# Second layer of a four-layer kernel: a quarter of the row maxima from half sums and half differences of the keys

## What is computed

```python
x_n = layernorm(x) * ln_gamma + ln_beta
q, k, v = split(x_n @ W_qkv + b_qkv)            # 16 heads of 8
scores = einsum('bhqd,bhkd->bhqk', q, k) * SCALE
scores = scores - max(scores, axis=-1)
attn = exp(scores)
attn = attn / maximum(sum(attn, axis=-1), 1e-12)
out = einsum('bhqk,bhkd->bhqd', attn, v) @ W_proj + b_proj
```

## Time and profile before

| | us |
|---|---|
| median of three runs | 3675.79 (3672.70 to 3679.34) |
| profiled execution, its own time | 3687.74 |
| its span in the profile | 3685.8 |
| `project` of the second layer, first load to barrier | 912.1 to 976.7 |
| slots ahead of the first step | 976.7 to 1028 |
| interleaved steps of the second layer | 1028 to 1686 |

### The profile page before, as it was taken

One profiled execution on the slowest core, in us unless ns is written; L12 is line 12 of the kernel. 1 busy time (PEld: TensorE's weight loads), 2 busy tenths in 40 slices (PEclk: granted clock), 3 DMA queues, 4 the chain that ended last, 5 costly groups with the idle time before them and its releaser, 6 DMA issues. The chain is left out here.

```text
span 3685.8 us, 51694 instructions
## 1 busy us (share of the span) xinstructions
PE 3002.9 (81%) x18320; PEld 1216.2 (33%) x18320; DVE 2627.6 (71%) x6022; ACT 2152.2 (58%) x2736; POOL 454.1 (12%) x601
## 2 busy tenths in 40 slices
PE   2699998787699999996599989986458988989836
PEld 1133333343212222223355555554332222222214
DVE  4688884456699999984566666641578888888831
ACT  2266665221267777785255545442259999989822
POOL 3000000323200000000000000002231010101023
PEclk9699998898689999998699999987779999999968
DMA  6422320422521121100000000011264222221102
GB/s 238 123 47 49 51 33 5 89 47 50 184 50 30 35 39 30 30 2 4 30 1 1 1 7 1 7 52 41 72 150 57 32 28 31 28 38 22 52 16 79
DMA packets 168110, 173.42 MB, mean 47 GB/s; under 512 B 46648, under 2 KB 126280, under 8 KB 165296
## 3 DMA queue, kind: packets, MB, share of 16 engines
q1 hardware_dynamic: 163760, 162.38, 20.2%
q0 software_dynamic: 4096, 7.78, 0.6%
HBM read 107.71 MB, written 62.26 MB: 46 GB/s over the span
## 5 line engine op out<-in xcount | busy, mean ns | idle before, releaser
L1205 ACT ACTIVATE a_probs<-a_scores 128x1024 f32<-128x1024 f32 (+3 forms) x896 | 793.1, 934 | 386.1 <-PE a_scores L1102 228.8
L1228 DVE TENSOR_REDUCE a_part_max<-a_slot_ps 128x1 f32<-128x512 f32 x1280 | 798.5, 683 | 44.9 <-PE a_slot_ps L1080 43.8
L1080 PE MATMUL a_slot_ps<-a_k_op,a_q_op 48*128 48x512 bf16 (+3 forms) x1792 | 585.4, 380 | 122.9 <-DMA a_mask_wide<-in_mask_wide 32.3
L2225 DVE TENSOR_TENSOR a_probs<-a_logit_ps,a_gate 128x1024 f32<-128x1024 f32 x512 | 602.4, 1219 | 102.6 <-ACT a_gate L2084 97.1
L2089 ACT ACTIVATE a_probs<-a_probs 128x2048 f32<-128x2048 f32 x256 | 488.0, 1906 | 9.4 <-DVE a_probs L2225 7.8
L1102 PE MATMUL a_scores<-a_q_op,a_k_op 51*128 51x512 bf16 (+3 forms) x1792 | 439.7, 362 | 18.5 <-ACT a_probs L1205 16.0
L1122 PE MATMUL a_o_ps<-a_probs,a_v_op 128*32 128x512 f32 (+3 forms) x3584 | 438.7, 561 | 1.2 <-ACT a_o_sb L1192 0.6
L1080 PEld LDWEIGHTS a_slot_ps<-a_k_op,a_q_op 48*128 48x128 bf16 x1792 | 149.7, 94 | 682.3 <-DVE a_part_max L1228 471.6
L1990 PE MATMUL a_logit_ps<-space 96*128 96x512 bf16 x1024 | 302.7, 386 | 75.3 <-DVE a_probs L2225 65.6
L2084 ACT ACTIVATE a_gate<-a_diff_ps 128x1024 f32<-128x1024 f32 x256 | 261.4, 1021 | 58.4 <-PE a_diff_ps L1990 49.9
L2003 PE MATMUL a_o_ps<-a_probs,a_v_op 128*32 128x512 f32 x2048 | 274.9, 608 | 7.0 <-DVE a_o_sb L2218 3.1
(11 more groups left out here) (389 smaller groups left out, 3791.1 us busy)
## 6 DMA issues: line engine op xcount, KB each, us to landing
scratch_v<-p_vpad SPq DMA_DIRECT2D x16, 1024.0 KB, 7.6
a_v_op<-scratch_v SPq DMA_DIRECT2D x32, 512.0 KB, 6.0
e_coef<-coef_dram SPq DMA_DIRECT2D x16, 1024.0 KB, 9.7
a_q_op<-scratch_q SPq DMA_DIRECT2D x384, 32.0 KB
a_k_op<-scratch_k SPq DMA_DIRECT2D x384, 32.0 KB
scratch_q<-p_parts SPq DMA_DIRECT2D x24, 384.0 KB, 4.5
scratch_k<-p_parts SPq DMA_DIRECT2D x24, 384.0 KB, 5.1
space<-scratch_k SPq DMA_DIRECT2D x192, 32.0 KB
```

What stands on the lines that cost most here:

```text
L1080: nc.tensor.matmul(out[:, 0:width], q_op[g][r0:r0 + MAX_ROW, e, qt * P:(qt + 1) * P], k_op[g][r0:r0 + MAX_ROW, e, kh * CH:kh * CH + width] ...
L1205: nc.scalar.activation(probs[gs % NB][:, 2 * e:2 * e + 2, off:CH], scores[e][:, :, off:CH], ACT.Exp, scale=scale).then_inc(probs_done, 1)
L1228: nc.vector.tensor_reduce(part_max[u % 2][:, kh, col:col + 1], slot[:, 0:w], axis=AX.X, op=ALU.max).then_inc(slot_done, 1)
L2225: nc.vector.tensor_tensor(probs[gs % 4][:, m, :, :], logit_ps[m][:], gate[gs % 2][:], op) \
```

## The change

In 8 of the 32 row tiles of a unit (odd head of the pair, odd `qt`; so slots B and D of every second group) the two slots are no longer the scores against the two halves of the keys. `project` computes two more operands for each batch element, (k of half 0 + k of half 1)/2 and their half difference, by two accumulating matmuls each with the k weights times 0.5 and -0.5, splits them into three parts like k and stores them in `scratch_halves`. `load_qk` loads them, 12 more DMAs for a unit. Slot B is now queries by half differences; ScalarE writes its absolute value to `sizes` in SBUF and frees the bank (`size_done`), VectorE passes over it. Slot D is queries by half sums; VectorE adds the sizes and takes the maximum in one `tensor_tensor_reduce`. The larger of two numbers is their half sum plus the size of their half difference, so the maximum over 1024 keys is the same. The first layer passes no `halves` and keeps its instructions, but for a wider preset of `part_max` and one wait in `project` that names a later chunk.

```diff
+    items = [(c, kind) for c in range(CHUNKS) for kind in ("qksd" if halves is not None and c % 2 else "qk")]
...
+                    else:
+                        te.wait_ge(halved, 2)
+                        nc.tensor.matmul(item_ps[n % NB][:], w_half[0][:], xnT[(c - 1) % 4][:], start=True, stop=False)
+                        nc.tensor.matmul(item_ps[n % NB][:], w_half["sd".index(kind)][:], xnT[c % 4][:], start=False, stop=True) \
+                            .then_inc(item_ready, 1)
...
+            if self.halves is not None:
+                for i in range(2):
+                    src = self.halves[b, i, kp, g * 32:(g + 1) * 32, :].rearrange("(e h r) t -> h r e t", e=2, h=2)
+                    r0 = HALF_ROWS + n * 8
+                    sp.dma_start(self.k_halves[g][r0:r0 + 8, i, :, :], src[1, :, :, :]).then_inc(self.qk_loaded[g], 16)
...
             def bank_for(n):
                 if n >= BANKS:
-                    te.wait_ge(slot_done, n - BANKS + 1)
+                    apart, count = shape.released[n - BANKS]
+                    te.wait_ge(size_done if apart else slot_done, count)
...
+            def slot_sizes(todo):
+
+                for u, s in todo:
+                    n = shape.place["slot", u, s]
+                    apart, count = shape.released[n]
+                    if apart:
+                        act.wait_ge(slot_ready, n + 1)
+                        if count > 2:
+                            act.wait_ge(slot_done, shape.released[shape.place["slot", *pairs[count - 3]]][1])
+                        nc.scalar.activation(sizes[(count - 1) % 2][:], slot_ps[n % BANKS][:], ACT.Abs).then_inc(size_done, 1)
...
                     for e in range(2):
+                        slot_sizes(todo[cut[2 * e]:cut[2 * e + 1]])
                         act.wait_ge(scores_ready, gs * 2 + e + 1)
...
+                        slot_sizes(todo[cut[2 * e + 1]:cut[2 * e + 2]])
...
+                if shape.in_pair(s):
+                    count = pairs.index((u, s)) + 1
+                    dve.wait_ge(size_done, count)
+                    nc.vector.tensor_tensor_reduce(out=slot[:], in0=slot[:], in1=sizes[(count - 1) % 2][:], scale=1.0,
+                                                   scalar=-3e38, op0=ALU.add, op1=ALU.max,
+                                                   accum_out=part_max[u % 2][:, kh, col:col + 1]).then_inc(slot_done, 1)
+                    return
```

More of the change, by code:

```diff
@@ L162, in _ @@
                 b, half = c // 2, c % 2
-                for i in range(ITEMS):
-                    n = c * ITEMS + i
+                for n in of_chunk[c]:
+                    kind = items[n][1]
+                    if kind in "qk":
+                        dram = (qs if kind == "q" else ks)[b, :, :, half * CH:(half + 1) * CH]
+                    else:
+                        dram = halves[b, "sd".index(kind)]
                     sp.wait_ge(lo_done, n + 1)
-                    sp.dma_start((qs, ks)[i][b, :, :, half * CH:(half + 1) * CH].rearrange("k f t -> f k t"),
-                                 parts[n % (2 * NB)][:]).then_inc(stored[n % (2 * NB)], 16)
+                    sp.dma_start(dram.rearrange("k f t -> f k t"), parts[n % (2 * NB)][:]).then_inc(stored[n % (2 * NB)], 16)
                 sp.wait_ge(v_done, c + 1)
@@ L171, in _ @@
                 if c == 3:
-                    for i in range(4):
-                        sp.wait_ge(stored[i], 16)
+                    for n in of_chunk[0] + of_chunk[1]:
+                        sp.wait_ge(stored[n], 16)
                 if c >= 3:
@@ L176, in _ @@
             for i in range(2 * NB):
-                sp.wait_ge(stored[i], 16 * (CHUNKS * ITEMS // (2 * NB)))
+                sp.wait_ge(stored[i], 16 * (len(items) // (2 * NB)))
             for i in range(4):
@@ L259, in _ @@
                 nc.gpsimd.memset(vp[:, :, :, hd:hd + 1], 1.0).then_inc(v_preset, 1)
-            for n in range(CHUNKS * ITEMS):
+            if halves is not None:
+                pool.wait_ge(loaded, 16 * n_loads)
+                for i, factor in enumerate((0.5, -0.5)):
+                    nc.gpsimd.tensor_scalar(w_half[i][:], w_qk[1][:], factor, None, ALU.mult).then_inc(halved, 1)
+            for n in range(len(items)):
                 pool.wait_ge(mid_done, n + 1)
@@ L899, in __init__, with in_pair, apart @@
         self.n = len(self.steps)
-        self.place = {}
+        self.place, self.released = {}, []
+        count = {False: 0, True: 0}
         for key in self.slot_order():
             self.place[key] = len(self.place)
+            apart = key[0] == "slot" and self.apart(key[2])
+            count[apart] += 1
+            self.released.append((apart, count[apart]))
+    def in_pair(self, s):
+        j, qt, kh = self.slots[s]
+        return not self.causal and j % 2 == 1 and qt % 2 == 1
+    def apart(self, s):
+        return self.in_pair(s) and self.slots[s][2] == 0
     def off(self, hq, kb):
@@ L963, in __init__ @@
         self.v_loaded = [nc.alloc_semaphore(f"{name}_v_loaded{i}") for i in range(GROUPS)]
-        self.qs, self.ks, self.vs = qs, ks, vs
+        self.qs, self.ks, self.vs, self.halves = qs, ks, vs, halves
+        self.loads = 4 * len(PAIR_PARTS)
+        if halves is not None:
+            self.k_halves = [sb(f"k_halves{i}", [P, 2, 2, CH], BF16) for i in range(GROUPS)]
+            self.loads += 2 * len(PAIR_PARTS)
     def load_qk(self, sp, u, parts=range(len(PAIR_PARTS))):
@@ L1023, in narrow_attention @@
         block = ctx.enter_context(nc.Block())
-        N_QK, N_MAX = 4 * len(PAIR_PARTS), 6
+        N_QK, N_MAX = operands.loads, 6
+        pairs = [key[1:] for key in shape.place if key[0] == "slot" and shape.in_pair(key[2]) and not shape.apart(key[2])]
         def column_of(j, qt):
@@ L1079, in a_slot @@
                 width = shape.slot_width(s)
-                nc.tensor.matmul(out[:, 0:width], q_op[g][r0:r0 + MAX_ROW, e, qt * P:(qt + 1) * P],
-                                 k_op[g][r0:r0 + MAX_ROW, e, kh * CH:kh * CH + width], start=True, stop=True).then_inc(slot_ready, 1)
+                keys = k_op[g][r0:r0 + MAX_ROW, e, kh * CH:kh * CH + width]
+                if shape.in_pair(s):
+                    keys = operands.k_halves[g][r0:r0 + MAX_ROW, 1 - kh, e, :]
+                nc.tensor.matmul(out[:, 0:width], q_op[g][r0:r0 + MAX_ROW, e, qt * P:(qt + 1) * P], keys,
+                                 start=True, stop=True).then_inc(slot_ready, 1)
             def max_turn(u):
@@ L1196, in _ @@
                     off, gs = shape.off(hq, kb), u * S + n
+                    todo = shape.ahead(u, n)
+                    cut = [len(todo) * p // 4 for p in range(5)]
                     if n == 1 and u > 0:
```

74 lines of the change are left out of this document (45 added, 29 removed).

## The result

The changed kernel takes 3681.05 us (median of 20 runs) against 3675.36 for the kernel before (20 runs): 1.0015 times as long, 95% interval 1.0008 to 1.0022. That is 5.7 us more, between 3 and 8. The forecast was 3686, 10.4 us more.

The account below looks back on a forecast made before the run. The prediction took a circle of waits through TensorE's order to bound the attention steps and DMA the projection; 13 - 3.6 + 0 + 1 = +10.4 us on 3675.8 gave 3686, range 3677 to 3704.

Parts of the forecast that it names:

- The bound of the steps: Second layer's attention steps: a loop of waits through TensorE's order sets the 2.49 us, not VectorE's 2.40 us of reductions.
- The circle of 2.49 us: Attention steps: reduction A, D's weight load, values, next A's load and matmul, back to reduction A; pieces sum to 2.49 us.
- Gain in the steps 0: Attention steps: VectorE has 0.55 us less to do in an even step, yet the step gets no shorter.
- The cost of the new wait 0: Even attention steps: D's add-and-maximum waits for Abs on ScalarE, but this fits without lengthening the step.
- The predicted slack: Even attention steps: VectorE is free at L + 2.85, the next A ready at L + 2.91 (L: A's load), 0.06 us to spare.
- Step 10, +1: Unit's last slot D, before the maxima are merged: add-and-maximum ends about 0.07 us later, for 15 units, +1 us.
- ScalarE's tables: ScalarE in the attention steps: Abs between Exps needs no table load; the rival with two loads a pair had chance 0.02.
- Slots ahead, -3.6: Slots before the first attention step: 0.36 us saved for each of 10 pairs, -3.6 us, bounds 0 and -5.5.
- Projection, +13: Block ahead of the attention, bound by DMA: 10.7 us for 3.34 MB plus half of 4.4 for early loads; bounds 9 and 16.
- DMA engines busy throughout: Sign expected in the profile after: projection block's barrier about 13 us later, with its DMA engines never short of work.
- The compute of the added items, 0: Projection block: work for 8 added items, 16 us at most, hides in the 26 us when engines stand idle.
- slower by over 0.2%: Whole kernel: slower by more than about 7 us, what a measurement can tell from no change; chance 0.69.

Follow-up runs that it names:

- attention only: Changed kernel without the added stores in the projection, operands of slots B and D loaded from k itself (maxima not right): 3673.0 us, 0.9985 against the kernel before.

## Why the prediction was right, point by point

- **The bound of the steps.** Right. The circle of 2.49 us holds A's reduction and no other: cut there, the kernel gains 69 us, cut at C, 4. VectorE spared a tenth of its work outside the circle gave 0.9986. The Trainium skill ("Perfetto Trace Analysis", Identifying the Most-Contended Engine) names the engine with the highest occupancy as the one to optimise first, and calls occupancy a fair measure of how close VectorE is to the roofline. By that VectorE was first here, at 98.6%; the measurement decides against the rule.
- **Gain in the steps 0.** Right: 657.3 and 657.6 us.
- **The cost of the new wait 0.** Right, but by luck. Abs is 0.59 long and starts 1.56 behind A's load, both as foreseen. But D starts 0.15 after Abs ends (1326.94 to 1327.09), not 0.04, and the next reduction starts 0.61 after it, not 0.65. The predicted slack was 0.06 us; VectorE is free at the moment when the next A is ready (1327.70), and the doubled Abs, paid in full in the plain steps, shows that there is none. The two errors add up to just the slack.
- **Step 10, +1.** Steps 10 and 11 together are 0.01 longer in the trace: 0.2 us, too small to matter.
- **ScalarE's tables.** No load between Exp and Abs: Exp 1 starts 0.48 after Abs (1326.35 to 1326.83). The Trainium skill ("ScalarE: Activation LUTs", Table sets) puts abs in every set, and the trace agrees.
- **Slots ahead, -3.6.** Right: -3.7. The bank of C is the limit, as worked out: in the trace C starts 0.78 us after A (1031.18 to 1031.96), where VectorE alone would need 0.60. (The prediction's terms sum to 0.775, not to the 0.79 it states.) VectorE alone would have gained 5.5.
- **Projection, +13.** Right in the sum (+12.1), wrong in its parts. The stores cost 8.4 us, where 10.7 were counted for stores and the bytes of the loads (10.1 for the stores alone): 3.15 MB in 8.4 us are 375 GB/s, what the DMA engines move while stores are queued (376 from 936.4 to 941.4), and the mean of 312 GB/s that I divided by also holds the slow stretches of the early loads. The early loads cost 4.2, not 2.2: as much as all 12 x 0.35 us of their issue time, with none of it hidden. The forecast's sign "DMA engines busy throughout" did not hold there: 0.71 and 173 GB/s from 951.4 to 956.4.
- **The compute of the added items, 0.** Right, though not by much: TensorE now works to 960 and GpSimd into the seventies, with the block ending at 987.
- **The total.** 10.4 forecast, 8.7 in the traces, 5.7 (3 to 8) in the timed runs. So the added time was forecast at nearly twice its size; the range of 3677 to 3704 was wide enough to hold 3681. The timed runs also give less than the traces' sum, by 3 us here and by 6 for attention only, and no stretch that the change touches accounts for it. What is behind the last step took 1988 to 2000 us in the four profiles of kernels built on the one before (mean 1993) and 1985 to 1990 in the nine built on the changed one (mean 1987). That has the sign and the size of what is missing, but with one profile a kernel it may be chance, and the cause stays open. Of the chances given, 0.69 lay on slower by over 0.2%; it is slower by 0.15%, which the text called within.

## What to carry to other kernels

An engine's busy share of 99% doesn't make it the bound: look for the one gap in its period that is longer than the others, follow the release that ends it around until it closes, and add the pieces; if they sum to the period, only what is in the circle counts. Before taking work off an engine, cut the same amount at a place in the circle and at one outside; the two times say where to work. And a bank freed earlier by a copy on an engine with room can be worth more than arithmetic saved on a busy one, whose added operands have to be stored and loaded besides.

## What the runs showed of the hardware

- The add-and-maximum with its accumulator's read-out lets the next reduction start 0.61 to 0.62 us after its own start, the read-out (0.14 us) lying beside it: nearly as short as a plain reduction of 128x512 (0.60), with twice the operands. With Abs twice, where the next A is long ready (loaded at 1347.70), it is 0.62 (1347.79 to 1348.41), so this is VectorE's own time.
- From the end of Abs to VectorE's D it took 0.14 to 0.15 us, but to TensorE's next load 0.05 (with Abs twice: Abs ends at 1347.65, the load of A is at 1347.70, D at 1347.79). VectorE to TensorE took 0.05 (reduction A to D's load) and TensorE to VectorE 0.04.
- Small loads on SyncE's queue (0.35 us of issue each) ahead of stores in the same queue cost as much as their whole issue time, 4.2 us for 12, although the DMA engines are busy 87.6% from 927 to 976.6 us in the kernel before.
